# Four layer normalisations of a four-layer block: pipelined over sequences, scaled on ScalarE

## The reference

```python
def _layernorm(x, axis=-1, eps=1e-05):
    m = jnp.mean(x, axis=axis, keepdims=True)
    v = jnp.var(x, axis=axis, keepdims=True)
    return (x - m) / jnp.sqrt(v + eps)
...
    xn = _layernorm(x, axis=-1)
    s = _L2_attn_ref(xn, ...)
    g = _silu(_L2_ffn_ref(xn, ...))
    x = x + s * g
```

## Time and profile before

| | us |
|---|---|
| runs, median of three | 4585.36 |
| lowest and highest | 4571.75, 4590.67 |
| the profiled execution | 4551.75 |
| its span, first to last instruction | 4550.0 |

### The profile page before, as it was taken

One profiled execution on the slowest core, in us unless ns is written; L12 is line 12 of the kernel. 1 busy time (PEld: TensorE's weight loads), 2 busy tenths in 40 slices (PEclk: granted clock), 3 DMA queues, 4 the chain that ended last, 5 costly groups with the idle time before them and its releaser, 6 DMA issues. The chain is left out here.

```text
span 4550.0 us, 93172 instructions
## 1 busy us (share of the span) xinstructions
PE 3573.2 (79%) x30644; PEld 2174.7 (48%) x30644; DVE 2631.0 (58%) x5893; ACT 1955.8 (43%) x3783; POOL 1259.7 (28%) x1828
## 2 busy tenths in 40 slices
PE   4699999759994799942999943547987379999997
PEld 1244444337762122221677721126986246666664
DVE  5576777541115677745677763862743656666664
ACT  3366666413333477721333321312323245565662
POOL 0011111100000111100677730611532534444440
PEclk9799999859996799965999966558769679999999
DMA  3322222100001211100665501102000233333330
GB/s 94 81 57 55 58 54 58 27 10 6 14 1 45 55 45 42 43 3 17 174 159 160 158 33 43 35 28 64 3 3 15 63 98 118 113 115 118 111 118 24
DMA packets 197623, 286.62 MB, mean 63 GB/s; under 512 B 40609, under 2 KB 154728, under 8 KB 196978
## 3 DMA queue, kind: packets, MB, share of 16 engines
q1 hardware_dynamic: 193270, 274.87, 21.6%
q0 software_dynamic: 4096, 8.40, 0.8%
HBM read 229.14 MB, written 35.72 MB: 58 GB/s over the span
## 5 line engine op out<-in xcount | busy, mean ns | idle before, releaser
L679 ACT ACTIVATE att_E<-att_pX,att_gs 128x512 f32<-128x512 f32 (+3 forms) x1024 | 722.8, 740 | 409.9 <-PE att_pX L613 176.4
L716 DVE TENSOR_REDUCE att_mx<-att_pS 128x1 f32<-128x512 f32 (+4 forms) x960 | 730.0, 787 | 290.1 <-PE att_pS L587 186.6
L1863 POOL TENSOR_TENSOR att_E<-att_E,att_rz 128x128 f32<-128x128 f32 (+3 forms) x512 | 357.6, 719 | 436.4 <-DVE att_rz L2071 436.4
L582 PE MATMUL att_pS<-att_ks,att_qs 72*128 72x512 bf16 (+4 forms) x1536 | 409.6, 339 | 79.8 <-DMA att_ks<-parts 56.4
L607 PE MATMUL att_pX<-att_qs,att_ks 75*128 75x512 bf16 (+4 forms) x1536 | 421.4, 329 | 30.3 <-ACT att_E L679 15.4
L1573 POOL TENSOR_TENSOR pairs_h<-pairs_m,pairs_r 128x512 f32<-128x512 f32 x272 | 345.7, 1271 | 354.5 <-DVE pairs_m L1636 344.6
L1597 PEld LDWEIGHTS pairs_po<-pairs_a,pairs_h 128*128 128x128 f32 x2176 | 286.6, 192 | 131.0 <-issue 129.0
L545 POOL CAST att_mp<-att_m 16x128 bf16<-16x128 f32 x288 | 80.5, 279 | 942.0 <-DVE att_m L727 916.8
L624 PE MATMUL att_pO<-att_E,att_vs 128*9 128x512 f32 (+3 forms) x3072 | 321.0, 490 | 1.3 <-ACT att_E L679 1.3
L1618 ACT ACTIVATE pairs_r<-pairs_ph 128x512 f32<-128x512 f32 x272 | 162.4, 597 | 332.2 <-PE pairs_ph L1589 332.2
L2002 ACT ACTIVATE att_E<-att_S,att_nm 128x128 f32<-128x128 f32 (+3 forms) x512 | 282.0, 556 | 39.9 <-DVE att_nm L2065 39.6
(11 more groups left out here) (406 smaller groups left out, 6645.3 us busy)
## 6 DMA issues: line engine op xcount, KB each, us to landing
pairs_c<-weights SPq DMA_DIRECT2D x272, 256.0 KB, 3.9
att_bias<-in_bias_dram SPq DMA_DIRECT2D x64, 896.0 KB, 4.6
parts<-proj_part SPq DMA_DIRECT2D x144, 128.0 KB, 2.3
att_xb<-xnT SPq DMA_DIRECT2D x64, 256.0 KB, 2.6
att_qs<-parts SPq DMA_DIRECT2D x192, 64.0 KB
att_ks<-parts SPq DMA_DIRECT2D x192, 64.0 KB
att_w<-in_w3a_dram SPq DMA_DIRECT2D x64, 192.0 KB, 2.4
att_qs<-parts SPq DMA_DIRECT2D x96, 96.0 KB
```

The lines of the kernel that those rows point to most:

```text
L582: ins = nc.tensor.matmul(pS[:, bank, n * w:(n + 1) * w], qs[:K1, u, x, q * P:(q + 1) * P], ks[:K1, u, x, :w], start=(n == 0 or not causal) ...
L679: nc.scalar.activation(E[:, kt % 2, WIDE * xp:WIDE * (xp + 1), :w], places(c)[0], ACT.Exp, scale=gs[:, g % 2, gain_of:gain_of + 1]).then_i ...
L716: V.reduce_max(dst, src, AX.X).then_inc(s_mx, 1)
L1863: nc.gpsimd.tensor_tensor(E[:, k, :width(j)], E[:, k, :width(j)], rz[:, u, k:k + 1].broadcast_to([P, width(j)]), ALU.mult).then_inc(s_n, 1)
```

## The change

`norm_phase` is written anew; nothing else in the kernel is touched.

- All loops are written out. DVE runs a pipeline over blocks of tokens: the statistics of block n (`variance`), then the small work of block n-1 (`offset`), then, in norm2, that of block n-2 (`offset2`).
- The two 128x512 passes over the tile on DVE are gone. DVE computes one number per token, `nb = -mean * rs`, with one 128x4 instruction, and ACT computes `x * rs + nb` with four 128x128 activations, whose scale and bias are columns of `rs` and `nb`. In norm2 their output goes to `R.s` itself, so the copy is gone as well.
- `ex` has three buffers, and ACT takes a silu two blocks ahead.
- In norm2 the second variance is derived: the variance of `xn` is `var * rs * rs`. Its rsqrt comes from a second power on POOL, and the second version is formed from `x` with the factors `rs * rs2` and `nb * rs2`: two of its four groups on ACT, two on DVE. It has PSUM buffers of its own.
- Statistics and factors have a buffer for each block of tokens. The waits of DVE on its own semaphore became drains.

```diff
             @block.gpsimd
...
+                for n in range(B + 1):
+                    if n < B:
+                        pool.wait_ge(s_var, n + 1)
+                        nc.gpsimd.tensor_tensor(rs[:, n], ve[:, n], half[:, :], ALU.pow).then_inc(s_rs, 1)
+                    if second and n:
+                        pool.wait_ge(s_var2, n)
+                        nc.gpsimd.tensor_tensor(rs2[:, n - 1], ve2[:, n - 1], half[:, :], ALU.pow).then_inc(s_rs2, 1)
             @block.scalar
...
+                def silu(n):
+                    if n >= 3:
+                        act.wait_ge(s_cmb, n - 2)
+                    nc.scalar.activation(ex[:, n % 3], flat(R.f, n), ACT.Silu).then_inc(s_silu, 1)
+                def norm(n):
+                    act.wait_ge(s_nb, n + 1)
+                    if store is None and n >= 2:
+                        act.wait_ge(s_pT, n - 1)
+                    for j in range(QT):
+                        ins = nc.scalar.activation(normed(n)[:, j], R.x[:, n * QT + j], ACT.Identity, bias=nb[:, n, j:j + 1], scale=rs[:, n, j:j + 1])
+                    ins.then_inc(s_xn, 1)
...
+                for n in range(B + 3):
+                    if combine and n + 2 < B:
+                        silu(n + 2)
+                    if n < B:
+                        norm(n)
+                    if 0 <= n - 1 < B:
+                        leave(n - 1)
+                    if second and 0 <= n - 1 < B:
+                        norm2(n - 1)
+                    if second and 0 <= n - 2 < B:
+                        leave2(n - 2)
             @block.vector
...
-                            c.link(nc.vector.tensor_tensor(dst[:, u], src, mv[:, u, :, 0:1].broadcast_to([P, QT, D]), ALU.subtract))
-                            dve.wait_ge(s_rs, scaled(dve, n, NV, v + 1))
-                            nc.vector.tensor_tensor(dst[:, u], dst[:, u], rs[:, u].rearrange("p (a o) -> p a o", o=1).broadcast_to([P, QT, D]),
-                                                    ALU.mult).then_inc(s_xn, 1)
...
+                def variance(n):
+                    if combine:
+                        e = ex[:, n % 3]
+                        dve.wait_ge(s_silu, n + 1)
+                        then(V.tensor_tensor(e, e, flat(R.s, n), ALU.mult))
+                        V.tensor_tensor(flat(R.x, n), e, flat(R.x, n), ALU.add).then_inc(s_cmb, 1)
+                        dve.drain()
...
+                    V.tensor_scalar(ve[:, n], mv[:, n, :, 1], EPS, None, ALU.add).then_inc(s_var, 1)
+                def offset(n):
+                    dve.wait_ge(s_rs, n + 1)
+                    V.scalar_tensor_tensor(out=nb[:, n], in0=mv[:, n, :, 0], scalar=-1.0, in1=rs[:, n], op0=ALU.mult, op1=ALU.mult).then_inc(s_nb, 1)
+                    if second:
+                        then(V.tensor_tensor(ve2[:, n], mv[:, n, :, 1], rs[:, n], ALU.mult))
+                        then(V.tensor_tensor(ve2[:, n], ve2[:, n], rs[:, n], ALU.mult))
+                        V.tensor_scalar(ve2[:, n], ve2[:, n], EPS, None, ALU.add).then_inc(s_var2, 1)
+                def offset2(n):
+                    dve.wait_ge(s_rs2, n + 1)
+                    V.tensor_tensor(rsb[:, n], rs[:, n], rs2[:, n], ALU.mult)
+                    then(V.tensor_tensor(nb2[:, n], nb[:, n], rs2[:, n], ALU.mult).then_inc(s_nb2, 1))
+                    if n >= 2:
+                        dve.wait_ge(s_pM, n - 1)
+                    for j in range(QT // 2, QT):
+                        ins = V.tensor_scalar(xm[:, n % 2, j], R.x[:, n * QT + j], rsb[:, n, j:j + 1], nb2[:, n, j:j + 1], ALU.mult, ALU.add)
+                    ins.then_inc(s_xmD, 1)
+                for n in range(B + 2):
+                    if n < B:
+                        variance(n)
+                    if 0 <= n - 1 < B:
+                        offset(n - 1)
+                    if second and 0 <= n - 2 < B:
+                        offset2(n - 2)
```

More of the change, by code:

```diff
@@ new lines, in leave, with norm2 @@
+                def leave(n):
+                    act.wait_ge(s_pT, n + 1)
+                    nc.scalar.activation(seq(R.xnT, n), pT[:, n % 2], ACT.Copy).then_inc(s_xT, 1)
+                def norm2(n):
+                    act.wait_ge(s_nb2, n + 1)
+                    if n >= 2:
+                        act.wait_ge(s_pM, n - 1)
+                    for j in range(QT // 2):
+                        ins = nc.scalar.activation(xm[:, n % 2, j], R.x[:, n * QT + j], ACT.Identity, bias=nb2[:, n, j:j + 1], scale=rsb[:, n, j:j + 1])
+                    ins.then_inc(s_xmA, 1)
@@ new lines, in leave2 @@
+                def leave2(n):
+                    act.wait_ge(s_pM, n + 1)
+                    nc.scalar.activation(seq(R.xn2T, n), pM[:, n % 2], ACT.Identity, bias=second[1], scale=second[0]).then_inc(s_xM, 1)
+                if combine:
+                    silu(0)
+                    silu(1)
+                for n in range(B + 3):
[9 more added lines that the diff above has]
+                        leave2(n - 2)
@@ L151, in _ @@
             @block.tensor
             def _(pe):
-                def body(i, first, last):
-                    for u in range(2):
-                        n = i * 2 + u
-                        for v in range(NV):
-                            pe.wait_ge(s_xn, scaled(pe, n, NV, v + 1))
-                            if not (first and u * NV + v < 2):
-                                pe.wait_ge(s_xT, scaled(pe, n, NV, v - 1))
-                            for j in range(QT):
-                                ins = nc.tensor.transpose(pT[:, (v + u * NV) % 2, j * P:(j + 1) * P],
-                                                          (xm if v else xn)[:, u, j], R.ident[:, :])
-                            ins.then_inc(s_pT, 1)
@@ L165, in _ @@
-                run_bodies(pe, B // 2, body)
+                for n in range(B + 1):
+                    if n < B:
+                        pe.wait_ge(s_xn, n + 1)
+                        if n >= 2:
+                            pe.wait_ge(s_xT, n - 1)
+                        for j in range(QT):
+                            ins = nc.tensor.transpose(pT[:, n % 2, j * P:(j + 1) * P], normed(n)[:, j], R.ident[:, :])
+                        ins.then_inc(s_pT, 1)
+                    if second and n:
+                        m = n - 1
+                        pe.wait_ge(s_xmA, m + 1)
+                        pe.wait_ge(s_xmD, m + 1)
+                        if m >= 2:
+                            pe.wait_ge(s_xM, m - 1)
+                        for j in range(QT):
+                            ins = nc.tensor.transpose(pM[:, m % 2, j * P:(j + 1) * P], xm[:, m % 2, j], R.ident[:, :])
+                        ins.then_inc(s_pM, 1)
```

101 lines of the change are left out of this document (24 added, 77 removed).

## The result

| | us |
|---|---|
| the kernel before beside it, median of four | 4586.28 (4571.75 to 4590.67) |
| the changed kernel, median of four | 4467.19 (4450.34 to 4490.13) |
| ratio | 0.9741, 95% interval 0.9719 to 0.9763 |
| the changed kernel's profiled execution, its span | 4490.13, 4487.8 |

The sign, the place and the kind of work were right. The term that had decided between the forecast and the first rival was not, and the comparison holds some 19 us that don't come from the normalisations. Neither alone takes the time out of the range: with the 100 us by which the stretches shrank in place of 88, the forecast from the median would have been 4485.

A forecast was written before the change was run, and what follows sets the result against it. A chain through the engines, not any engine's work, was taken to bound the four normalisations. Savings of 12.3 + 17.5 + 41.1 + 17.2 = 88 us from the median 4585.4 gave 4497 us, range 4470 to 4526.

The forecast's parts named there:

- the first rival: Normalisations: POOL's power frees the port early, so DVE is not held; gain 103.5 us, 4482 us; chance 0.38.
- What bounds the kernel: Four normalisations, 233.3 of 4550 us: a chain through the engines bounds them, and a microsecond saved there shortens the span.
- the very thing that the prediction said would speak against it: Sign outside the normalisations: the prediction is wrong if the matmul phases change their length.
- DVE's block of 3.15 us: Norm1 and norm3: DVE needs 3.15 us per block of tokens after the change, 3.78 if held by the power.
- ACT's four activations: Scaling on ACT: 0.39 us per activation, four 1.56 us a block; norm0 then bound by ACT at 2.06.
- I take 0.63: Norm1 and norm3: POOL's power holds DVE's addition to `x`, 0.63 us a block, bounds 0 and 1.38.
- The tails: Work after the last block's variance: 5.1 us in norm1, 7.0 us in norm2.
- I subtract from the median: Whole kernel: the 88 us come off the median 4585.4, not the profiled 4551.75, giving 4497 instead of 4464.
- The rule against ScalarE: Multiply and add belong on VectorE by the skill; by it only norm0 would lose some gain, about 4 us.
- ACT as the bound everywhere: Rival 2, normalisations: activations of 0.48 us and late waits make ACT the bound; gain 60, 4525 us; chance 0.14.
- TensorE's clock: Rival 3, matmul stages: shorter rests lower the clock; 2.5% costs 89 us, 3.5% gives 4622 us; chance 0.03.

The follow-up runs named there:

- the three repeats: The changed kernel run again, unchanged, beside the kernel before: 4443.77, 4453.32 and 4449.86 us (ratios 0.9766, 0.9772, 0.9778).
- Experiment 4: Changed kernel with an unused POOL product of 128x512 ahead of the power in blocks 1 to 7 of norm1 and norm3: 4465.23 us, ratio 0.9806.
- the first comparison: The changed kernel, unchanged, against the kernel before, four runs each: medians 4467.19 and 4586.28 us, ratio 0.9741.
- the seven kernels of the table: Changed kernel with POOL reading long, scaling on DVE, no lag, second statistics, interleaved DVE, silu three ahead, or added ACT copies: 4438.32 to 4559.89 us.
- the two pairs: Both kernels with the gather moved behind the output phase (before 4633.46, changed 4525.82 us), or its eight loads issued first (before 4550.99, changed 4453.70 and 4448.54).
- Experiment 5: Changed kernel with the scaling of norm0, norm1 and norm3 as four DVE instructions per block instead of four on ACT: 4469.22 us, ratio 0.9811.

## Why the prediction was wrong

- **What bounds the kernel: right.** The gain lies in the four stretches, since phases meet at their ends. Outside them the first pair of profiles differs by 38 us, the very thing that the prediction said would speak against it; 34 of them are one execution's output phase, and the three repeats don't show them.
- **DVE's block of 3.15 us: right, as long as nothing holds it.** Blocks last 3.09 (line 210 at 1361.21 and 1364.30); one block of norm1 has a gap of 0.43 whose end the trace ascribes to no event. From the first product to the last variance norm1 takes 24.9 us, forecast 25.1 without the holding.
- **ACT's four activations: right.** The copy starts 23.57 - 22.03 = 1.54 us behind the first of four, 0.385 from start to start, forecast 0.39. Norm0 became ACT's with 2.01 us a block, forecast 2.06.
- **"I take 0.63": the step that failed.** The forecast added 0.63 us a block for an addition held by the power, and 1.0 in norm2. The runs show zero: 16 additions of 0.69 us with the power beside them, and in norm2 lines 217 and 201 at their own length. I had read the exclusion from instructions that go through 512 columns or more and carried it to one with four columns. Experiment 4 shows where it does hold. The term was 4.4 + 6.6 + 4.4 = 15 of the 88 us; its bound of 0 gives the first rival, 103.5, against 100.0 measured in the stretches. The sentence ahead of the choice named the reason to doubt it (a fraction of 0.87 us), and 0.38 against 0.45 was as near as I stood. The Trainium skill ("SBUF — State Buffer", Who interferes with whom) lets the first to issue keep the shared pair for its whole instruction; experiment 4's 1.37 us agrees, the power beside 16 additions doesn't, and the measurement decides.
- **The tails: too short.** Norm1's was 5.1 and is 1379.32 - 1373.58 = 5.7; norm2's was 7.0 and is 10.5, because ACT has a backlog of two blocks when DVE is done. That is the 3 us by which the first rival missed norm2, and it hid half of the wrong holding there: 6.6 too little gain against 3.5 too much.
- **"I subtract from the median": a second size.** The kernel before lay 34 us above its profiled execution in the runs shown, and the changed one gained 119 there. On three chips later the gain was 101 to 110 with the same stretches. The kernel before ran 32 us slower in the first comparison than later, the changed one only 14 to 23. Its profiled execution, 4551.75, lies among the later runs and below all four of the first comparison, so the 34 us were no property of the kernel, and the forecast started from a median that held them. In the seven kernels of the table with other lengths, medians follow stretches within 3 us; in the changed one's repeats and the two pairs they lie 1 to 10 us beyond; the part behind norm3 can be 2 to 4 us of that. The rest of the 19 us of the first comparison is of its chip or its executions; which, stays open.
- **The rule against ScalarE.** The prediction weighed the Trainium skill's advice ("ScalarE: Activation LUTs", Rules for kernel authors) at a loss of 4 us at most. Experiment 5 is that advice followed: DVE is faster at it, 1.11 against 1.65, and the three stretches are 16 us longer, since DVE bounds norm1 and norm3, and becomes the bound of norm0.
- **The rivals.** ACT as the bound everywhere: not so, it waits for DVE in norm1 (0.45 us a block). TensorE's clock: the mean granted clock was 0.865 in the changed kernel's first profile and 0.869 to 0.873 in the repeats, 0.862 before. That mean rises by itself when stretches at the lower level get shorter; what speaks against a loss is PE's busy time, 3573 and 3567 us before, 3563 to 3570 in the repeats (3584 in the first profile), where the rival had 89 us more.

## What to carry to other kernels

When two engines exclude each other over memory, look at how much data each goes through, not at how long each lasts: an instruction of four columns that went on for 0.87 us held nobody here, one of 512 columns did. Before shortening the list of the engine that bounds a pipeline, follow who must deliver earlier for it, for a ring through a second engine can cost more than the gaps held; one buffer more, and the silu a block earlier, opened it here. And where phases meet at their ends, compare stretches, which repeated within 0.2 us, before medians, whose difference moved between 101 and 119 for the same two kernels.

## What the runs showed of the hardware

- A POOL power on 128x4 takes 1.01 us alone and 1.45 behind a DVE instruction on two 128x512 tiles, of which it ends 0.86 to 0.87 after; a DVE addition of two 128x512 tiles beside it keeps its 0.69, and a DVE product of 128x4 its 0.17.
- A POOL product of 128x512 beside the same addition makes it 1.37, and the addition then ends 0.55 after POOL's.
- DVE instructions that read one tile leave the power its 1.01: statistics already running when it starts, and a scaling with two numbers per partition (128x128, four in 1.11) that starts behind it.
- Loads issued by SyncE kept DVE waiting 32 us in one of four profiles of the changed kernel; the wait ended 2.6 us after the last of the gather's 64 indirect DMAs had been issued. Why they were late was not shown.
